# A decoder layer on one core: feed-forward weights summed in self attention, quantised in cross attention, transposed by DMA at its end

## What is computed

```python
def _weight_quant(w):
    scale = 1.0 / jnp.clip(jnp.mean(jnp.abs(w)), 1e-05)
    return jnp.clip(jnp.round(w * scale), -1.0, 1.0) / scale
def _act_quant(x):
    scale = 127.0 / jnp.clip(jnp.max(jnp.abs(x), axis=-1, keepdims=True), 1e-05)
    return jnp.clip(jnp.round(x * scale), -128.0, 127.0) / scale
def _bitlinear(x, w):
    return jnp.einsum('bsi,oi->bso', _act_quant(x), _weight_quant(w))
x = _layernorm(x + _L0_attn_ref(x, ...), axis=-1)
x = _layernorm(x + _L0_xattn_ref(x, ctx_768, ...), axis=-1)
gate = jax.nn.silu(_bitlinear(x, w_gate)); up = _bitlinear(x, w_up)
x = _layernorm(x + _bitlinear(gate * up, w_down), axis=-1)
```

## Time and profile before

| what | us |
|---|---|
| runs | 2128.28, 2124.07, 2128.04 (median 2128.04) |
| profiled execution / its span | 2123.06 / 2121.4 |
| self attention | 0 to 642.6 |
| cross attention, to the barrier | 642.6 to 1864.4 |
| feed-forward until the first tile reaches POOL | 1864.4 to 1972.2 |
| feed-forward, the rest | 1972.2 to 2121.4 |
| busy PE / DVE / ACT / POOL | 1915.9 / 1523.4 / 1221.1 / 749.8 |
| DMA moved | 102.79 MB, mean 48 GB/s |

### The profile page before, as it was taken

How to read it: one execution, slowest core, us unless ns; L and a number is a source line. 1 busy time by engine, 2 the same in 40 slices (tenths; PEclk the granted TensorE clock), 3 DMA queues, 4 the chain that set the end, 5 groups by cost and what they waited for, 6 DMA issues and landing times. The chain is left out here.

```text
span 2121.4 us, 41377 instructions
## 1 busy us (share of the span) xinstructions
PE 1915.9 (90%) x13652; PEld 1611.0 (76%) x13668; DVE 1523.4 (72%) x3379; ACT 1221.1 (58%) x2644; POOL 749.8 (35%) x874
## 2 busy tenths in 40 slices
PE   5999989999985799999999988999999999727997
PEld 4777767777764799999999987999999999514443
DVE  4676766888864577777777776777777777557887
ACT  4657566575742456655656555566556655456664
POOL 0434324343440343433433333434343434300454
PEclk8999989999986899999999999999999999956999
DMA  3201021011104101110110121011101100060121
GB/s 97 84 26 52 26 73 47 27 44 34 35 26 134 38 26 46 43 31 30 39 48 26 39 81 37 23 48 38 35 22 48 40 25 0 18 251 20 55 72 57
DMA packets 56762, 102.79 MB, mean 48 GB/s; under 512 B 6192, under 2 KB 18192, under 8 KB 56192
## 3 DMA queue, kind: packets, MB, share of 16 engines
q1 hardware_dynamic: 51904, 91.56, 13.9%
q10 hardware_dynamic: 3840, 7.34, 1.1%
q0 software_dynamic: 960, 3.15, 0.4%
HBM read 83.68 MB, written 18.35 MB: 48 GB/s over the span
## 5 line engine op out<-in xcount | busy, mean ns | idle before, releaser
L1019 POOL TENSOR_TENSOR ca_pr<-ca_pr,ca_rec 112x750 f32<-112x750 f32 x256 | 364.9, 1441 | 527.7 <-DVE ca_rec L1348 527.7
L1249 ACT ACTIVATE ca_big_hi<-ca_ps_T 126x448 fp32r<-126x448 f32 x384 | 209.5, 546 | 147.2 <-PE ca_ps_T L1145 144.8
L1353 DVE TENSOR_TENSOR ca_big_lo<-ca_ps_T,ca_big_hi 126x448 fp32r<-126x448 f32 x384 | 238.2, 620 | 48.8 <-ACT ca_big_hi L1249 40.5
L314 POOL TENSOR_TENSOR sa_p_lo<-sa_pr,sa_p_hi 112x448 fp32r<-112x448 f32 x128 | 148.8, 1177 | 273.6 <-ACT sa_p_hi L495 273.5
L1145 PE MATMUL ca_ps_T<-ca_ident,ca_pr 112*126 112x112 f32 x1536 | 218.6, 265 | 17.2 <-DVE ca_big_lo L1353 17.0
L1145 PEld LDWEIGHTS ca_ps_T<-ca_ident,ca_pr 112*126 112x126 f32 x1536 | 165.4, 141 | 47.3 <-DVE ca_big_lo L1353 23.2
L1158 PE MATMUL ca_ps_O<-ca_big_hi,ca_v_st 126*128 126x224 f32 (+1 forms) x768 | 186.3, 284 | 1.4 <-DVE ca_big_lo L1353 1.4
L1158 PE MATMUL ca_ps_O<-ca_big_lo,ca_v_st 126*128 126x224 f32 (+1 forms) x768 | 180.2, 275 | 0.0
L1111 PE MATMUL ca_ps_P<-ca_w_hi,ca_ct_hi 128*126 128x256 f32 x576 | 173.1, 301 | 2.2 <-DVE ca_w_lo L1309 2.2
L366 PE MATMUL sa_ps_P<-sa_w_hi,sa_xt_hi 128*112 128x512 f32 x384 | 156.4, 407 | 14.2 <-DVE sa_w_lo L684 12.2
L1111 PE MATMUL ca_ps_P<-ca_w_hi,ca_ct_lo 128*126 128x256 f32 x576 | 162.9, 283 | 0.0
(11 more groups left out here) (246 smaller groups left out, 6207.6 us busy)
## 6 DMA issues: line engine op xcount, KB each, us to landing
ca_ctx_in<-in_ctx_dram SPq DMA_DIRECT2D x16, 567.0 KB
sa_xin<-in_x_dram SPq DMA_DIRECT2D x16, 448.0 KB, 3.6
ca_xin<-x SPq DMA_DIRECT2D x16, 448.0 KB, 3.5
ca_ctx_in<-in_ctx_dram SPq DMA_DIRECT2D x16, 378.0 KB
sa_stage<-in_L_attn_Wkv_dram SPq DMA_DIRECT2D x4, 1024.0 KB, 7.1
ff_raw<-in_L_ffn_w_gate_dram SPq DMA_DIRECT2D x2, 2048.0 KB, 12.1
ff_raw<-in_L_ffn_w_up_dram SPq DMA_DIRECT2D x2, 2048.0 KB, 19.6
ff_raw<-in_L_ffn_w_down_dram SPq DMA_DIRECT2D x2, 2048.0 KB, 7.4
```

Of the source, the lines that this page charges most:

```text
L314: pool.tensor_tensor(p_lo[:, h % NB, :], pr[:, h % NB, :], f32(p_hi[:, h % NB, :]), ALU.subtract).then_inc(p_split, 1)
L1019: pool.tensor_tensor(w, w, rec[:, h % PB, c:c + 1].to_broadcast([R, S]), ALU.mult).then_inc(norm_done, 1)
L1249: act.activation(weights_view(big_hi, h, t), blocks_view(u, t), ACT.Copy).then_inc(t_hi_done, 1)
L1353: dve.tensor_tensor(weights_view(big_lo, h, t), blocks_view(u, t), f32(weights_view(big_hi, h, t)), ALU.subtract).then_inc(drained[slot[u] ...
```

## The change

Self attention: in the first group, each step loads a piece of 128x1024 of each of the three matrices (`load_feed_forward`, 512 KB each), ACT takes magnitudes and sums (`add_magnitudes`, units `W0 W1 W2`), 24 instructions in all. At the end DVE adds the partial sums, PE totals them over partitions, and DVE makes mean and scale.

Cross attention: in 12 of the 16 steps (b below 6 of each group), for each of the three matrices, SP loads a chunk of 128x688 in f32 into `stage`, ACT scales and rounds it by adding a constant (unit `F`), DVE clips (unit `C`), ACT takes the constant off and writes bf16 (unit `G`), and SP stores the 128x688 in bf16 to DRAM. 36 chunks. The next chunk's load waits for the last one's store. SP's loops are unrolled. The first two weight chunks of the second group are loaded at b = 6, no more at the start. In the last step SP waits for the last ternary store and for the last drains of banks P0 and P1, and issues three transposing DMAs that bring the ternary matrices, 6.29 MB in all, to where the feed-forward stage uses them. They lie over buffers of cross attention that are no longer read (`w_hi0` to `w_lo2`, `stage`, `xin`). The block ends when they have landed.

PE's wait for a group's weights stands at `Y0` of each step, no more ahead of the group's loop. Feed-forward has no preparation of weights left.

```diff
-            ORDER = steps("""A2 A3 E2 L E3 P2 B0 P3 Q0+ A4 A5 E4 E5 B1 P4 A6 P5 E6 A7 P6 K0+ E7 P7 B2 B3 V0+ X++ ...
+            ORDER = steps("""A2 A3 E2 L E3 P2 B0 P3 W0 Q0+ A4 A5 E4 E5 B1 W1 P4 A6 P5 E6 A7 P6 K0+ E7 P7 W2 B2 B3 V0+ X++ ...
+            def add_magnitudes(m, b):
+                act.wait_ge(ff_loaded[m], counter(b, 0, B)(16, 16))
+                act.activation(ff_in[:, m, :], ff_in[:, m, :], ACT.Abs,
+                               accum_out=ff_part[:, m, bass.ds(b, 1)]).then_inc(ff_added, 1)
...
+            def load_feed_forward(s, m):
+                if m == 0 and s % WB == 0:
+                    sp.wait_ge(w_done, W * (s // WB + 1))
+                if s or m:
+                    sp.wait_ge(ff_out, 16 * (NW * s + m))
+                sp.dma_start(ff_chunk, ff_flat[m][:, ff_at[s]:ff_at[s] + WC]).then_inc(ff_in, 16)
+            def store_feed_forward(s, m):
+                sp.wait_ge(ff_done, NW * s + m + 1)
+                sp.dma_start(to_flat[m][:, ff_at[s]:ff_at[s] + WC], ff_small).then_inc(ff_out, 16)
...
+                    elif b == B - 1:
+                        sp.wait_ge(ff_out, 16 * NW * WB * GROUPS)
+                        for bank in ("P0", "P1"):
+                            sp.wait_ge(drained[bank], plan.uses[bank] * GROUPS * B + 1)
+                        for m, w in enumerate(ff_ternary):
+                            sp.dma_start_transpose(ff_held[m][:, :].rearrange("p (k r) -> p k r", r=w.shape[0]), w).then_inc(held, 16)
...
+            sp.wait_ge(held, 16 * NW)
             sp.wait_ge(stored, 16 * (GROUPS * B + 1))
...
+                        if name == "Y0":
+                            pe.wait_ge(w_done, W * (g + 1))
...
             for g in range(GROUPS):
-                pe.wait_ge(w_done, W * (g + 1))
...
+            def round_weights(m, at):
+                act.wait_ge(ff_in, at(16 * NW, 16 * (m + 1)))
+                act.activation(ff_chunk, ff_chunk, ACT.Copy, scale=ff_scale[:, m:m + 1], bias=ROUND).then_inc(ff_rounded, 1)
+            def ternary_weights(m, at):
+                act.wait_ge(ff_clipped, at(NW, m + 1))
+                act.activation(ff_small, ff_chunk, ACT.Copy, bias=-ROUND).then_inc(ff_done, 1)
+            ORDER = steps("""XT0+ XT1+ T3.0 CT00+ S4.1 Q0+ T3.1 CT01+ S5.1 O2 F0 T3.2 CT02+ CT10+ T4.0 CT11+ S6.0 O3 G0 T4.1 S7.0 V00+ V01+ T4.2
+                       V02+ S6.1 T5.0 S7.1 Q1+ Q2+ T5.1 F1 O4 CT12+ T5.2 K00+ K01+ G1 T6.0 K10+ T6.1 K11+ T6.2 O5 T7.0 S0.0+ K20+ K21+ T7.1 F2
+                       S1.0+ O6 V03+ T7.2 S0.1+ Q3+ G2 S1.1+ T0.0+ ...
...
+            def clip_weights(m, at):
+                dve.wait_ge(ff_rounded, at(NW, m + 1))
+                dve.tensor_scalar(ff_chunk, ff_chunk, ROUND - 1.0, ROUND + 1.0, ALU.max, ALU.min).then_inc(ff_clipped, 1)
...
             transpose_x(0)
-            pe.wait_ge(wt_copied, 2 * 2 * GROUPS_PER_HALF)
             gate_up(0, True, range(FB))
-            for half in range(2):
-                transpose_half(2, half)
-            pe.wait_ge(wt_copied, 3 * 2 * GROUPS_PER_HALF)
             transpose_x(1)
```

More of the change, by code:

```diff
@@ L8 @@
+import math
 from contextlib import ExitStack
@@ L98, in self_attention @@
     LN_LINKS = 3 + RSQRT_LINKS
+    NW = len(ff_weights)
+    ff_flat = [flat(w) for w in ff_weights]
+    WN = ff_flat[0].shape[1]
+    WC = WN // B
+    assert all(w.shape[1] == WN for w in ff_flat) and WN % B == 0
     assert GC == BANK and D == HALF and R <= P and NP == 4
@@ L463, in _ @@
                     step(b, g)
+            pe.wait_ge(made, 4)
+            pe.wait_ge(ff_summed, 1)
+            pe.wait_ge(drained["P0"], counter(B - 1, GROUPS - 1, B)(plan.uses["P0"], plan.uses["P0"] + 1))
+            pe.matmul(bank["P0"][:, 0:NW], ones[:, :], ff_sum[:, :], start=True, stop=True).then_inc(ff_total, 1)
         @block.scalar
@@ L1188, in do, with step @@
                     project_out(int(name[1]), at)
-            def step(at, ahead, weights=0):
+            def step(g, at, ahead, weights=0):
                 for name, next_batch in ORDER:
@@ L1292, in _ @@
             for g in range(GROUPS):
-                with act.Fori(0, looped(g)) as b:
-                    step(g, counter(b, g, B), counter(b, g, B, 1))
-                step(g, counter(B - 1, g, B), after(B - 1, g), g + 1 < GROUPS)
+                with act.Fori(0, WB) as b:
+                    step(g, counter(b, g, B), counter(b, g, B, 1), counter(b, g, WB))
+                for b in range(WB, B):
+                    step(g, counter(b, g, B), after(b, g), None, b == B - 1 and g + 1 < GROUPS)
                 if g + 1 < GROUPS:
@@ L1427, in _ @@
             for g in range(GROUPS):
-                with dve.Fori(0, looped(g)) as b:
-                    step(g, b, counter(b, g, B), counter(b, g, B, 1))
-                step(g, B - 1, counter(B - 1, g, B), after(B - 1, g), g + 1 < GROUPS)
+                with dve.Fori(0, WB) as b:
+                    step(g, b, counter(b, g, B), counter(b, g, B, 1), counter(b, g, WB))
+                for b in range(WB, B):
+                    step(g, b, counter(b, g, B), after(b, g), None, b == B - 1 and g + 1 < GROUPS)
                 if g + 1 < GROUPS:
@@ L1645, in _ @@
             pe.sem_inc(y_filled, 1)
[L1646 to L1665 removed]
+            pe.wait_ge(made, 5)
             def transpose_x(t):
@@ L1792, in _ @@
             silu(0, True, range(FB))
-            for half in range(2):
-                copy_weights(2, half)
             copy_x(1)
@@ L1947, in _ @@
                     quantise_x(1)
-            ternary(2, 1)
             dve.wait_ge(h_unit_clear, 1)
```

261 lines of the change are left out of this document (119 added, 142 removed).

## The result

The changed kernel takes 2093.47 us (median of 4, 2089.28 to 2096.78) where the one before took 2128.06: a ratio of 0.9841, 95% interval 0.9818 to 0.9863, or 34.6 us less. The prediction was 2100, 28 less. The profiled execution of the changed kernel is its longest, 2096.78 us with a span of 2095.0; that of the kernel before took 2123.06, 5.0 us less than its median. They explain these 26.4 us; where the other 8.2 us of the medians lie, no trace tells.

What follows compares the result with a forecast made beforehand. PE bounds cross attention; feed-forward waits for weight preparation, then POOL's layer norm and stores. -64 + 30 + 10 - 2 + 0 = -26 us gave 2100 us, own range 2085 to 2118, whole range 2064 to 2140.

Steps and rivals of the forecast that it cites:

- Feed-forward, -64: Start of feed-forward: without weight preparation the first three `gate_up` blocks come earlier, the rest stays bound by POOL; -64 us.
- Cross attention's passes, +30: Cross attention: new ACT and DVE passes delay PE by 2.5 us in each of 12 steps; +30 us, from +13 to +37.
- The slack ahead of PE's next transposes: Cross attention: time between DVE's low part and PE's next transposes; the part of a pass beyond it reaches PE.
- Self attention, +10: Self attention: W1 delays PE, +7 us in 8 steps; new loads queue in the first step, +3; from +3 to +17.
- PE's wait, -2: Group starts in cross attention: of the 7.9 us wait for weights about 6 stay, for a drained bank; -2 us, 0 to -4.
- The transposes, 0: End of cross attention: the transposing DMAs take 31 us, hidden under about 50 us of PE's work; 0 us.
- The price of 20 ns a piece: Transposing DMAs: 256-byte packets take 20 ns each, on the line between 4-byte and mean packets; 31 us in all.
- The rival at 140 us: Transposes priced as mean packets outlast the last step by 90 us: 2190; chance 0.16, including 0.03 block by block.
- the rival block by block: Each of 192 transposed blocks a transfer behind the last: 634 us, total 2684, or 2301 at 1309 ns; chance 0.03.
- The rival that the passes are covered: Cross attention: ACT's gaps take up the insertions and PE never sees them; 2062 us; chance 0.10.
- Late chunks: Cross attention: ACT or DVE waits 2 us for each of 36 chunk loads, PE with them; +72 us, 2172; chance 0.07.

Runs made afterwards that it cites:

- e7_moved: e6_moved_ca with the sums of self attention also moved, to places where ACT idles for PE: 2062.96 us, 0.9703 of the kernel before.
- e6_moved_ca: The changed kernel with the nine cross-attention passes of a step at other places, where ACT or DVE had idled: 2067.10 us, 0.9719 of the kernel before.
- e8: e7_moved with the last four weight chunks' splits inside each group's first step, feed-forward chunks in steps 1 to 6: 2039.00 us, 0.9593 of the kernel before.
- e2_wait_back: The changed kernel with PE's wait for a group's weights ahead of the group's loop again: 2101.07 us, 0.9872 of the kernel before.
- e3: The changed kernel with the three transposing DMAs issued behind the last store, not beside the last step: 2120.63 us, 0.9967 of the kernel before.
- e4: The changed kernel with the three transposes done twice, the second three when the first have landed: 2094.48 us, 0.9842 of the kernel before.
- e9_plain: The changed kernel with three plain DMAs of the same 6.29 MB in place of the transposing ones, output not the reference's: single run of 2097.86 us.
- e1_parts: The changed kernel with a different part of the new passes and sums left out in each step, loads and stores kept: one run, 2078.68 us.

## Why the prediction was right, step by step

- **Feed-forward, -64: right**, -64.6. The first `gate_up` came 7.0 us after the gate (7.8 said; DVE had the first tile of x 2.8 us after the gate, not 3.6), the next 12.3 and 13.2 behind each other (12.9 and 12.5). Everything behind stayed bound by POOL and its stores.
- **Cross attention's passes, +30: right in sum**, +27.4, and by chunk (1.35, 0.71 and 0.45 said; 1.30, 0.60 and 0.42 measured alone). By instruction it was wrong: alone F0, C0 and G0 cost 0.74, 0.79 and 0.20, where 0.46, 0.24 and 0.65 were said, and the third chunk's cost isn't at G2, which is free, but at F2 or C2, which the study didn't separate. That the chunk's sums fit all the same is luck. The slack ahead of PE's next transposes is the right quantity, but DVE's pass was 0.51 us, or 0.93 beside POOL, and not 0.46, and each delay was counted as if the others weren't there. POOL isn't in the forecast's price at all.
- **Self attention, +10: right**, +9.1, of it 4.1 for the W1 of five steps (0.8 each, 0.9 said) and 3.4 in the second step. There one sum waited 1.3 us for its load; the rest of the 3.4 isn't traced, but the step was 2.2 us shorter in e7_moved, with the sums elsewhere, than in e6_moved_ca.
- **PE's wait, -2: the mechanism right, the size not.** PE's new wait of 5.8 and 7.3 us for a drained bank was foretold, and e8 showed its cause, the splits ahead of the loops. But moving the wait gained some 5 us (e2_wait_back). The forecast took 7.9 less about 6, which is one group's start; there are two, and they gave 3.1 and 1.5 by the waits alone.
- **The transposes, 0: right.** 27 us against 31, and a cover of 50; e3 and e4 bound both. The price of 20 ns a piece, off a line between two packet sizes, was a guess that held (19.8 by the same formula). The rival at 140 us fell with the price of a small packet, the rival block by block with it: the figure of 1309 ns for a block in the Trainium skill (VectorE: DVE Perf Modes, section The three transpose paths) doesn't add up over blocks: 192 of them took 27 us. The Trainium skill's 261 GB/s (DMA: Bandwidth & Descriptors, section Latency and other measured facts) is near: 290 in most slices, and 233 GB/s for the 6.29 MB in 27 us with the slower stretches between the three.
- **The last two steps, +5.6 in the profiled execution: not in the forecast.** It is the clock; what lowered it stays open, and so does whether the faster executions have it. In the sum of cross attention it hides that the passes cost 2.6 less and the group starts 2.1 less than said: +28.9 against +28 is luck in part. By the medians the forecast was 6.5 us off, 2093.5 measured and 2100 said, which no trace divides.
- **The rival that the passes are covered fell for these places**, and e6_moved_ca shows that it is right for others. Late chunks: no pass waited.

## What to carry to other kernels

Work that is moved under another stage costs by its place: read the idle time ahead of each unit on the receiving engine in one steady step, and put each pass ahead of a unit that waits longer than the pass takes and that isn't on the way to the engine that bounds. When a pass goes on DVE, look at POOL's operations beside it too: the same pass took 0.51 us alone and up to 1.33 beside one. A wait that is moved on one engine only shows the next one, until the work that both stood for is moved too; here that was worth 18.9 us by the traces, where the wait alone had given 5. A transfer whose price no row shows can still be judged, if the cover it needs is read first.

## What the runs showed of the hardware

Three transposing DMAs of 2.1 MB each moved at 290 GB/s in most slices, in pieces of 256 bytes: 14.1 ns a piece and engine at that rate, while ordinary packets in the kernel before had a mean of 91 ns at 1.76 KB. So the number of pieces alone did not make these transfers dear. SP's queue was occupied by issuing them for 25 us (e3_late and e4_twice show the same, 24 and 25), and what stood behind them in that queue was issued after that; three plain DMAs of the same bytes occupied it for 1.3 us in e9_plain, and moved at up to 448 GB/s. Their queue from 1844 to 1885 us (packets, MB, share of 16 engines):

```profile
q1 hardware_dynamic: 432, 6.29, 37.9%
```

A pass of DVE over 128x688 from f32 to f32 took 0.51 us where no operation of POOL was running at its start. Where one was (L1123, 112x750 in f32, 1.44 us), the pass ended 0.37 us after POOL's did, however much of that was left: 0.89 us with 0.51 left (e1_parts), 0.93 with 0.55 (the changed kernel), 0.96 with 0.59 and 1.33 with 0.95 (e6_moved_ca). All passes of all runs lie within 0.01 us of the one or the other. The type written made no such difference: in the kernel before, DVE's passes over 128x4096 took 2.29 us to f32 (L1829) and 2.29 to bf16 (L1832).
